# Channel sums over 128 equal columns, a norm scale spread from a broadcast column, and the expert scaling on ScalarE

## What is computed

```python
x = x + conv(ln_c(x))          # norm over 256 channels; qkv 1x1, 5x5 depthwise, 1x1 grouped,
                               # linear attention (relu q, relu k), projection, batch norm
t = tokens(x)                  # 8 images, 1024 tokens, 256 channels
t = t + ffn(ln_t(t))           # norm over 256 channels
# ffn: per image a router (mean token -> 11 logits -> softmax -> top 2) gives 6 expert weights ew
# h = gelu(t @ W1[e] + b1[e]);  out = sum_e ew[e] * (h @ W2[e] + b2[e])
```

## Time and profile before

| | |
|---|---|
| median of 3 runs | 1725.85 us (1725.51 to 1727.48) |
| profiled execution | 1725.51 us, its span 1723.6 us |
| mean granted TensorE clock | 0.900 |
| PE, DVE busy | 1403.7 us (81%), 1303.4 us (76%) |
| POOL, ACT busy | 1187.4 us (69%), 915.0 us (53%) |
| chain that ended last | PE 44%, DVE 23%, POOL 16%, ACT 10%, issue 6% |

### The profile page before, as it was taken

One profiled execution on the slowest core, in us unless ns is written; L12 is line 12 of the kernel. 1 busy time (PEld: TensorE's weight loads), 2 busy tenths in 40 slices (PEclk: granted clock), 3 DMA queues, 4 the chain that ended last, 5 costly groups with the idle time before them and its releaser, 6 DMA issues.

```text
span 1723.6 us, 18116 instructions
## 1 busy us (share of the span) xinstructions
PE 1403.7 (81%) x6652; PEld 771.5 (45%) x6652; DVE 1303.4 (76%) x1305; ACT 915.0 (53%) x1606; POOL 1187.4 (69%) x1017
## 2 busy tenths in 40 slices
PE   4344865988889878988889878988889879768998
PEld 2133534544545435544545435544445435534443
DVE  4999999889589895889589895889589895920000
ACT  3452642565557644665557645565557645433554
POOL 3673554877697758876697758876697757535776
PEclk7666986999999989999999989999999989988999
DMA  5100000000010000100010000100010000100000
GB/s 173 74 0 25 1 0 0 25 1 13 1 62 1 13 1 0 62 1 13 1 60 3 13 1 1 61 1 13 1 37 1 13 0 1 37 0 13 1 13 25
DMA packets 14247, 32.70 MB, mean 19 GB/s; under 512 B 2384, under 2 KB 5328, under 8 KB 13904
## 3 DMA queue, kind: packets, MB, share of 16 engines
q1 hardware_dynamic: 14160, 31.56, 5.2%
HBM read 23.17 MB, written 8.39 MB: 18 GB/s over the span
## 4 chain that ended last, share of the span: by engine, by line
PE 44%; DVE 23%; POOL 16%; ACT 10%; issue 6%; DMA 1%; POOLq 0%; SPq 0%; DVEq 0%
DVE dacc L1067 19%; PE wbk L487 16%; PE acc L500 12%; PE wbk L580 6%; POOL dwo L881 4%; POOL gl L915 3%; POOL hb L912 3%; ACT tapb L655 2%; POOL yr L905 2%; PE wbk L589 2%; PE wbk L534 2%; POOL nrm L838 1%; PE wbk L539 1%; PE wbk L554 1%; PE wbk L566 1%
## 5 line engine op out<-in xcount | busy, mean ns | idle before, releaser
L1067 DVE SCALAR_TENSOR_TENSOR dacc<-qkvs,dww,dacc 128x930 f32<-128x930 f32 (+4 forms) x954 | 1052.3, 1185 | 0.0
L912 POOL TENSOR_SCALAR hb<-hb,ewg 128x512 f32<-128x512 f32 x256 | 189.8, 742 | 252.2 <-ACT gh L677 252.1
L915 POOL TENSOR_TENSOR gl<-hb,gh 128x512 f16<-128x512 f32 x256 | 306.3, 1196 | 21.4
L770 ACT ACTIVATE hb<-wbk,b1s 128x512 f32<-128x512 f32 x256 | 175.4, 686 | 244.4 <-PE wbk L487 243.8
L881 POOL TENSOR_TENSOR dwo<-dwo,tapb 128x992 f32<-128x992 f32 (+1 forms) x104 | 237.4, 2283 | 46.7 <-ACT tapb L655 39.5
L487 PE MATMUL wbk<-th,w1h 128*128 128x512 f16 x512 | 163.8, 403 | 69.7 <-ACT vt L743 36.7
L500 PE MATMUL acc<-gh,w2h 128*128 128x512 f16 x512 | 200.6, 392 | 19.4 <-POOL gl L915 19.3
L677 ACT ACTIVATE gh<-hb,ewg 128x512 f16<-128x512 f32 x256 | 182.3, 712 | 40.7 <-DVE ewg L1020 40.7
L500 PE MATMUL acc<-gl,w2h 128*128 128x512 f16 x512 | 200.0, 391 | 0.0
L500 PE MATMUL acc<-gh,w2l 128*128 128x512 f16 x512 | 199.8, 390 | 0.0
L487 PE MATMUL wbk<-tl,w1h 128*128 128x512 f16 x512 | 162.3, 400 | 0.0
(11 more groups left out here) (147 smaller groups left out, 2388.7 us busy)
## 6 DMA issues: line engine op xcount, KB each, us to landing
xa<-x SPq DMA_DIRECT2D x8, 1024.0 KB, 5.0
yr<-x SPq DMA_DIRECT2D x8, 1024.0 KB, 5.0
out<-yr SPq DMA_DIRECT2D x16, 512.0 KB, 2.8
dwo<-w SPq DMA_DIRECT2D x1, 2048.0 KB, 10.9
yr<-w SPq DMA_DIRECT2D x2, 1024.0 KB, 16.0
dwo<-w_qkv SPq DMA_DIRECT2D x1, 768.0 KB, 4.7
wp<-w_proj SPq DMA_DIRECT2D x1, 512.0 KB, 12.1
pw<-w_pw SPq DMA_DIRECT2D x16, 24.0 KB
```

What stands on the lines that cost most here:

```text
L770: last = nc.scalar.activation(hb[:, f % GB, :], b[:], ACT.Gelu, bias=b1s[:, f % FT:f % FT + 1], scale=1.0 / (X_SCALE * W_SCALE))
L912: nc.gpsimd.tensor_scalar(hb[:, f % GB, :], hb[:, f % GB, :], ewg[s % 2][:, f % FT:f % FT + 1], 0.0, ALU.mult, ALU.add).then_inc(g_scaled, 1)
L915: nc.gpsimd.tensor_tensor(gl[:, f % GB, :], hb[:, f % GB, :], gh[:, f % GB, :], ALU.subtract).then_inc(g_low, 1)
L1067: ins = nc.vector.scalar_tensor_tensor(out=dst[:, oy, ox], in0=i3[:, jy, jx], scalar=dww[:, m, tap:tap + 1], in1=a3[:, oy, ox], op0=ALU.mu ...
```

## The change

Four things are changed. The scaling of `hb` moves from POOL to ACT, directly behind gh. The sums use all 128 equal columns of `mean_w` as moving operand, so that each result is written 128 times, and the next one overwrites all but the first; both sums of both norms share one bank, half (STEP = 256 columns) for each. The diagonal on POOL is gone: the scale column is the stationary operand, repeated 128 times by its access pattern, and a diagonal `spread` (X_SCALE on the diagonal) the moving one. The two "stats" items of the first norm become one.

```diff
+STEP = CH // 2
@@ schedule
-            based([("stats", j + 1, 0, i) for i in range(2)])
+            based([("stats", j + 1, 0)])
@@ tensor
-                    L, i = it[2:]
-                    for q in ((i,), (0, 1))[L]:
+                    L = it[2]
+                    for q in range(2):
                         pe.wait_ge(summed[L], s * 2 + (q + 1))
                         data = rb[:, :] if q == 0 else nrm[:, 0, :]
                         for t in range(TT):
-                            last = nc.tensor.matmul(b[:, q * TT + t:q * TT + t + 1], data[:, t * P:(t + 1) * P],
-                                                    mean_w[:, 0:1], start=True, stop=True)
+                            last = nc.tensor.matmul(b[:, q * STEP + t:q * STEP + t + P], data[:, t * P:(t + 1) * P],
+                                                    mean_w[:], start=True, stop=True)
                 elif what == "rbc":
                     if c == 0:
-                        pe.wait_ge(diag_made[L], s + 1)
-                    last = nc.tensor.matmul(b[:], spread[:], rb[:, c * CH:(c + 1) * CH], start=True, stop=True)
+                        pe.wait_ge(ln_chain[L], s * 4 + 4)
+                    for t in range(c * (CH // P), (c + 1) * (CH // P)):
+                        o = (t - c * (CH // P)) * P
+                        last = nc.tensor.matmul(b[:, o:o + P], sv[L][:, 3, t:t + 1].to_broadcast([P, P]), spread[:],
+                                                start=True, stop=True)
@@ scalar
                     nc.scalar.activation(gh[:, f % GB, :], hb[:, f % GB, :], ACT.Copy, scale=w).then_inc(g_high, 1)
+                    nc.scalar.activation(hb[:, f % GB, :], hb[:, f % GB, :], ACT.Copy, scale=w).then_inc(g_scaled, 1)
...
+                    bt = b[:].rearrange("p (q n) -> p q n", n=STEP)
+                    last = nc.scalar.activation(st[it[2]][:], bt[:, :, 0:TT], ACT.Copy)
@@ gpsimd
-            after(nc.gpsimd.memset(spread[:], X_SCALE))
+            after(nc.gpsimd.memset(spread[:], 0.0))
+            after(nc.gpsimd.affine_select(out=spread[:], in_=spread[:], compare_op=ALU.not_equal, fill=X_SCALE, base=0,
+                                          pattern=[[-1, P]], channel_multiplier=1))
...
-                pool.wait_ge(ln_chain[L], s * 4 + 4)
-                nc.gpsimd.tensor_tensor(rb[:].rearrange("p (t n) -> p t n", n=P),
-                                        ident[:].unsqueeze(1).to_broadcast([P, TT, P]),
-                                        sv[L][:, 3, :].unsqueeze(2).to_broadcast([P, TT, P]),
-                                        ALU.mult).then_inc(diag_made[L], 1)
...
-                    pool.wait_ge(g_high, no)
-                    pool.sem_inc(pool_gate, 1)
-                    nc.gpsimd.tensor_scalar(hb[:, f % GB, :], hb[:, f % GB, :], ewg[s % 2][:, f % FT:f % FT + 1],
-                                            0.0, ALU.mult, ALU.add).then_inc(g_scaled, 1)
                     pool.wait_ge(g_scaled, no)
                     nc.gpsimd.tensor_tensor(gl[:, f % GB, :], hb[:, f % GB, :], gh[:, f % GB, :], ALU.subtract
```

More of the change, by code:

```diff
@@ L159, in schedule @@
         if c:
-            based([("stats", new, 1, 0)])
+            based([("stats", new, 1)])
             give(("rnorm", new, 1))
@@ L370, in build @@
         ln_chain = [sem(f"ln_chain{i}") for i in range(2)]
-        diag_made = [sem(f"diag_made{i}") for i in range(2)]
         normed = [sem(f"normed{i}") for i in range(2)]
@@ L814, in norm_scale @@
             def norm_scale(s, L):
-                pool.wait_ge(bank_drained, drained(("stats", s, L, 1 - L)))
+                pool.wait_ge(bank_drained, drained(("stats", s, L)))
                 m, q = st[L][:, 0, :], st[L][:, 1, :]
```

## The result

The changed kernel takes 1663.38 us in the median of four runs (1661.5 to 1666.14), the kernel before 1725.69 us (four runs): ratio 0.9638, 95% interval 0.9621 to 0.9655, so 62 us or 3.6% faster. The forecast was 1672 with a range of 1654 to 1702. The profiled execution took 1664.92 us (span 1663.2) against 1725.51.

What follows compares the result with a forecast made beforehand. No engine is full; an image is a cycle of waits between PE, ACT, POOL and DVE. Terms -32.5, -2.7, -22.8, +7.4, -1.8 and -1.5 sum to -53.9: median 1672 us, range 1654 to 1702.

Steps and rivals of the forecast that it cites:

- The stretch around ewg: From logits to attention: 6.8 less 0.3 for ACT's overruns, 6.5 us in five images, 2.7 in the first.
- The route's term: DVE's route from L986 to L1020: POOL's sums end earlier, so ewg comes 2.4 us earlier; ends 0 and 3.8.
- The term behind ewg: After ewg: rbc at 883.4 instead of 889.2, attention 5.6 us earlier, and PE's 1.22 us stall for gl goes too.
- Clock: PE's records slow after waits of 2.2 and 5.1 us, not after 1.86; half of the projection's 1.6 us counted.
- Channel sums: PE's sums with 128 columns instead of one: +0.3 us, on PE's path for the second norm only; ends 0 and +0.44.
- Base taps: Between 926 and 996 POOL's adds end earlier, PE's waits shrink to 3.1 and 1.2 us: 3.8 us in six images.
- the fourth rival: More clock: all of the projection's 1.6 us, and before L534 too; 21 us more gain, 1651 us; chance 0.10.
- Costs on ACT: The new activation, 0.61 us a block, overruns ACT's idle time: per image 0.3 tokens, 0.35 burst, 0.2 an attention half.
- The second: Sums or gls move but still cover the route, clock still falls before the projection: 17 us less gain, 1689; chance 0.26.
- The third: ACT becomes the bound, its extra 0.61 us landing on PE's path; 1782 us at 24 of 32 blocks; chance 0.06.
- The fifth: PE from projection to logits and then DVE set the image, relief is swallowed: about 1724 us, no change; chance 0.04.
- Start and end: At the start L828 is exposed, 1.8 us gained; at the end two waits for a scaling before the last products, 1.5.

Runs made afterwards that it cites:

- the three orders above: The changed kernel as it is, with the router's exponentials ahead of the next image's squares, and with squares and sums one fill earlier: 1663.38, 1660.07 and 1662.31 us.
- The last run: Changed kernel with the router's exponentials ahead of the squares, and the second norm's squares and sums behind the first two token items and their fill: 1644.37 us.
- the exponentials first: Changed kernel with the router's exponentials ahead of the squares of the next image instead of behind them: 1660.07 us.
- each half alone: Kernel before with only the scaling of hb moved to ACT: 1690.38 us; changed kernel with that scaling back on POOL: 1692.01 us.

## Why the prediction was right, and where it was not

**The stretch around ewg** (forecast 6.5 an image, of it 2.4 for the route and 3.4 behind it). Measured 1.98, 3.32 and 0.76 before agg: 6.1. L998 and L995 became short as said, and the stall moved to L987. The route's term is right in size and reason: with the scaling alone the route is 2.0 shorter, and rbc comes 1.9 sooner after mx. The term behind ewg is right in size and not in reason. It was to come from POOL's relief and the merged item, with full clock behind the sums taken for granted. But the scaling alone left this stretch at 8.7 us, and the changed kernel with one column has 8.17: of the 3.32 won, 2.84 hang on the 128 columns, to which the forecast gave only a cost. That this size came out is luck. And ewg still earlier brings nothing more: the three orders above have the same image.

**Clock.** I read from the earlier trace rows that a wait of 1.86 us leaves the clock alone and one of 2.2 does not. That step failed. The same 2.22 us went both ways in one kernel, and 1.31 us ahead of one-column sums was followed by the 1.2 GHz level. The pair with one and 128 columns shows that what PE does after the wait counts, and the two images with 2.22 that the place in time does; no run here shows by which rule.

**Channel sums** (forecast +0.3 us an image, ends 0 and +0.44). As a duration this is right: 3.57 us against 3.46. As a term of the sum it has the wrong sign. The columns are worth 18 us in the kernel before and 23 in the changed one. For the kernel before, part of that is the arrival at the projection, as said. I had the row in hand: the earlier trace rows shows one-column and 128-column records at nearly the same length, and I asked only what the longer ones cost, not what the shorter ones do to the clock.

**The last image** (forecast 0, measured 4.0). Of this, 3.2 lie between the start of the sums behind the last projection and rbc (13.7 and 10.5 us): before, the granted clock was 0.58 in the first half of them and 0.50 in the second and for some 4 us behind; now, behind the same wait of 4.64, it comes back in their second half:

```profile
1572.26 6.48 PE wbk L589 x32
```
```profile
1575.20:1578.70 3.50, 3.50 (x18) 3.50 (x19) 0.00 (x0) 0.00 (x0) 0.00 (x0) 0.50 0.00 0
```
```profile
1515.80 5.44 PE wbk L590 x32
```
```profile
1518.00:1521.50 3.50, 3.50 (x23) 3.26 (x22) 0.00 (x0) 0.18 (x1) 0.00 (x0) 0.73 0.00 0
```

(The first two are of the kernel before, the last two of the changed one; the chain, then busy time by stretch.)

**Base taps** (forecast 3.8, with 1.15 of costs against it). From agg to mx the image is 4.1 shorter. The parts differ: the wait before L534 is 4.46, not 3.1, that before the projection 0.64, not 1.2, and the projection runs at full clock in all of its records, which was the fourth rival's price. That rival's other half, L534 at full clock, did not come. The wait before L534 shrank by 0.65, not by 2.0, because of a term that the forecast had at nothing: the POOL add that ACT awaits is not only free to start earlier, it now takes 3.27 us, in all six images, where it took 2.29. It starts while DVE's tap L1055, which reads two SBUF operands, still runs, and the 1.0 us more is about what was left of that tap. First POOL of the kernel before, then POOL and DVE of the changed one:

```profile
951.04 2.29 POOL L881 TENSOR_TENSOR dwo<-dwo,tapb 128x992 f32<-128x992 f32 x1
```
```profile
917.97 3.27 POOL L881 TENSOR_TENSOR dwo<-dwo,tapb 128x992 f32<-128x992 f32 x1
```
```profile
915.02 4.08 DVE L1055 SCALAR_TENSOR_TENSOR dacc<-qkvs,dww,dwo 128x1024 f32<-128x1024 f32 x2
```

With the scaling alone, agg to mx is 3.5 shorter, so this term does come from POOL's relief, within its costs.

**What bounds the kernel.** The walk through the image found hardly a gap of PE from 844 to 860, from 903 to 926 and at the projection, and did not look between 801 and 844. There stood a wait of 5.16 us for a drain, as long as the longest one it named. The last run won some 15 us at that place (1644.4 against 1660.1 with the exponentials first).

**Costs on ACT** (0.3 for tokens, 0.35 for the burst, 0.2 for attention). A kt drain is 0.08 later than before. The total of ACT's cost cannot be read apart from the gains. That the first activation is worth moving is shown by the 35 us of the scaling alone, and that a second one is not free by the 89 us.

**Rivals.** The second (1689) kept "the route still covered" and "the clock still falls". Of the first half a part came true: POOL still holds the route up by 1.6 and 1.0 us, yet it is 2.0 shorter. The second half did not come. The third did not come at this load; with 0.7 us more on ACT its mechanism did. The fifth did not come: each half alone gave over 30 us.

**Start and end** (1.8 and 1.5). Measured 1.7 and 0.7.

**The sum.** Forecast 53.9, measured 60.6. Undone one by one in the changed kernel, the columns cost 23.0, the diagonal 20.6, the scaling 28.6 and the second bank item 5.7, together 78: the parts overlap. Several of them guard the same full clock, which may be why; no run separates that. The sign was sure for the reason given, relief of POOL; that, the diagonal and the merged item, without the columns, are 39 us, 15 less than forecast. So the forecast came close because a gain that it did not see, 23 us by the columns, outweighed what it had too high; the time without the columns, 1686, would still lie in its range.

## What to carry to other kernels

When PE's short products stand next to its waits, ask what they do to the granted clock before asking what more columns cost: here 32 products of 128 equal columns took 0.1 us longer than 32 of one column and saved 18 to 23 us. Judge work moved to another engine by what is queued behind it in that engine's order: moving 0.61 us per block to ACT won 35 us, and 0.7 more per block cost 89. And after a gain read all waits anew: the route, which the change made 2 us shorter, gave nothing more when it was made shorter still, while an order of two items on ACT, untouched by the change and there from the start, was worth some 15.

## What the runs showed of the hardware that was not expected

The granted clock does not follow from the length of a wait: 2.22 us ahead of the projection gave 0.50 in one image and 1.00 in the next, in one kernel. It depends on what PE does: behind 1.31 us, sums of one column were followed by 0.50 and sums of 128 columns by 1.00, though PE loaded weights without a gap in both. The Trainium skill (TensorE: Matmul & The Clock Gate, Part 1: The HAM clock gate) says that the chip's observation of PE runs freely and does not start with the kernel's work, so that the point of a change varies. The two images agree with that; no run here shows where its limits fall.

Of DVE's short instructions, the cast (1.73 instead of 0.17 us), TENSOR_SCALAR (2.23 instead of 0.23) and a TENSOR_TENSOR of two SBUF operands (1.40 instead of 0.41) were held until POOL's instruction ended, and RECIPROCAL (0.16) was not. The Trainium skill (SBUF — State Buffer, SBUF: two separate sides) gives the lock to VectorE's instructions in a two-port mode or with two SBUF inputs; that agrees, and is narrower than the rule as the prediction told it. In which mode an instruction ran no view shows, so for the cast and TENSOR_SCALAR the agreement is only that these were held and RECIPROCAL was not. The other direction shows too: POOL's add took 3.27 us instead of 2.29 where it started during a DVE tap with two SBUF operands.
